# Expert stage of a top-4 mixture: output stores move from ScalarE's DMA queue to SyncE's, TensorE reads its expert numbers per product group, loop bodies go from 48 to 24 steps

## The chip, the cores and the metric

The kernel runs on one core of a Trainium2 chip. The metric is the device time of one execution in microseconds (us); the figure that counts is the median of several runs. TensorE is called PE in the profile, VectorE DVE, ScalarE ACT, GpSimd POOL and SyncE SP; a "q" behind a name (SPq, ACTq) is that engine's queue of DMA instructions.

## The reference

The input is 8 sequences of 1024 rows of 256 numbers, 8192 rows in all. What is computed, cut to its core:

```python
x = x + time_and_channel_mix(layernorm(x))            # first half, 16 tiles of 512 rows
xt = layernorm(x).reshape(-1, 256)                     # 8192 rows
gates = sigmoid(xt @ expert_sel.T)                     # 32 experts
val, idx = top_k(gates, 4)
scores = relu(einsum('nd,edf->nef', xt, keys)) * gate_full[:, :, None]    # keys: 32 x 256 x 128
out = einsum('nef,efv->nv', scores, values)            # values: 32 x 128 x 256
return x + out
```

The first half is a layer norm, a recurrence over the rows of a sequence with four 256x256 projections, an output projection, a second norm and a two-layer mix of width 1024. The kernel computes the products of each row for its four chosen experts only.

## The kernel before

**The mixing stage** works through 16 tiles of 512 rows. Each engine has a list of its own for a tile; four tiles are written out, then a loop of two tiles per pass runs five times, then the rest is written out. At the end of each tile POOL scatters the 512 x 4 rows (each row to four experts) with 16 indirect DMAs (L1340) into `lists`, a table in DRAM in which each block of 128 rows ("unit") belongs to one expert. DVE keeps the plan: which expert each unit has (`plan_expert`), and, for the first 48 units, which are worked off in another order, where they lie (`plan_row`) and where their results go (`plan_store`).

**The expert stage** is `expert_phase` (from L1396). 288 units are taken two at a time, which makes 144 steps; one step's 256 rows are a batch. All five engines run the same step list, each shifted:

- SP loads batch i at its step i (`rows`, L1474): 256 KB from `lists` to one of six homes `xr`. In the first 24 batches (the head) it reads two row numbers from `plan_row` into registers (L1457) and issues two DMAs of 128 KB (L1479); later it issues one DMA (L1483). Ahead of that it waits until DVE has finished step i-6 (L1501). SP also loads the residual tiles (`load_resid`, L1486) and stores the finished tiles (`store_tile`, L1492), one of each per 8 steps.
- PE at its step i does the first product of batch i-2 (`inner`, L1553: eight matmuls against `keys`), transposes batch i (`turn_rows`, L1575), transposes the hidden rows of batch i-4 (`turn_sums`, L1588) and does the second product of batch i-6 (`outer`, L1597: six matmuls against `values`). Which expert's weights these use comes out of `plan_expert` through registers: `experts_of` (L1540) reads them for four steps at a time, eight registers, once for the keys and once for the values. Both reads of four steps fall in the same step.
- ACT waits for PE's step (L1660) and then copies four results out of PSUM: L1663, L1666 (`xt_hi`), L1669, and L1676, which writes the output `y` of batch i-6 into one of four homes. At the start of its next step it stores that batch (`store`, L1642): in the head two register reads and two DMAs of 128 KB (L1648), later one DMA of 256 KB (L1651), all on ACT's own DMA queue. Before L1676 it waits until the batch four earlier has landed in `sorted_rows`.
- DVE has three instructions per step (L1717, L1720, L1726), of which L1720 (`xt_lo`) allows PE the first product two steps on, and from step 36 on two weighted sums (L1707) per step. Four groups of 128 rows, eight steps, make one output tile.
- POOL gathers, per tile, 16 times 128 rows of `sorted_rows` (L1758), four for each group of 128 rows. It starts on tile n when batches up to 8n+23 have landed (L1753), and for each group waits until DVE has summed the group four earlier (L1755), since `ye` has four homes.

The loops: SP, ACT, PE and DVE each write out 48 steps, then loop over 48 steps twice, then write out the rest:

```python
SPAN = 6 * RING                                   # RING = 8
for i in range(SPAN): step(i, i % SPAN, i // SPAN)
with pe.Fori(1, NSTEPS // SPAN) as pair:          # NSTEPS = 144
```

POOL's list has no loop here.

Of the kernel before, what the change touches and what calls it, by code (L numbers as in the profile page):

```python
# [44 lines left out]
UNIT = P  # L45
# [26 lines left out]
SUM_LAG = 36  # L72
OUT_AT = SUM_LAG + RING + HOMES[0] * WIDE
RESID_AT = OUT_AT - 20
PLAN_STEP, FIRST_RESIDS, KEYS_FIRST = 2, 14, 7
OPEN_BELOW = (UNIT - 1) / UNIT

# [1318 lines left out]
def expert_phase(nc, scope, sem, g):  # L1396
# [32 lines left out]
    (pe_step, low_ready, xhi_ready, x_ready, sums_ready, hhi_ready, h_ready, ycopy_ready, sum_step) = (  # L1429
        sem(n) for n in "pe_step low_ready xhi_ready x_ready sums_ready hhi_ready h_ready ycopy_ready sum_step".split())  # L1430

    SPAN = 6 * RING
    BATCHES = SPAN // WIDE
    HEAD_BATCHES = HEAD_END // FOLD
    SUM_END = SUM_LAG + 2 * NT * J
    HELD = 4
    PART_OF = P // FOLD
    assert NSTEPS % SPAN == 0 and SPAN % HELD == 0 and SPAN // RING % RESIDS == 0 and HEAD_END <= SUB * SPAN
    assert all(BATCHES % homes == 0 and HEAD_BATCHES % homes == 0 for homes in (XB, YB))

    def within(i, first, end):

        return not isinstance(i, int) or first <= i < end

    def in_head(b):

        return isinstance(b, int) and b < HEAD_BATCHES
# [25 lines left out]
    def on_sync(sp):  # L1473
        def rows(b, r):  # L1474

            q = r % XB
            if in_head(b):
                for n, at in enumerate(held_rows(sp, plan_row, b * FOLD, LIST_ROWS - UNIT)):
                    sp.dma_start(xr[n * PART_OF:(n + 1) * PART_OF, q],  # L1479
                                 lists[bass.ds(at, UNIT), :].rearrange("(p f) d -> p f d", f=FOLD)  # L1480
                                 ).then_inc(rows_loaded[q], 16)
            else:
                sp.dma_start(xr[:, q], lists[bass.ds(b * (FOLD * UNIT), FOLD * UNIT), :]  # L1483
                             .rearrange("(p f) d -> p f d", f=FOLD)).then_inc(rows_loaded[q], 16)

        def load_resid(tile, q, nth):  # L1486

            after(sp, out_stored[q], 16 * nth)
            sp.dma_start(resid[:, q], residual[bass.ds(tile * TILE, TILE), :].rearrange("(p j) d -> p j d", j=J)
                         ).then_inc(resid_loaded[q], 16)  # L1490

        def store_tile(tile, q):  # L1492

            sp.wait_ge(sum_step, TOPK * J * (tile + 1))
            sp.dma_start(out[bass.ds(tile * TILE, TILE), :].rearrange("(j p) d -> p j d", p=P), resid[:, q]
                         ).then_inc(out_stored[q], 16)

        def step(i, r, pair):
            if r % WIDE == 0 and within(i, 0, NSTEPS):
                b = BATCHES * pair + r // WIDE  # L1500
                after(sp, x_ready, i - (XB - 1) * WIDE)  # L1501
                rows(b, r // WIDE)
            for at, act_on in ((OUT_AT, store_tile), (RESID_AT, load_resid)):
                if (r - at) % RING == 0 and within(i, at, at + NT * RING):
                    n = (r - at) // RING
                    tile, q, nth = (SPAN // RING) * pair + n, n % RESIDS, (SPAN // RING // RESIDS) * pair + n // RESIDS
                    if act_on is store_tile:
                        store_tile(tile, q)
                    elif not (isinstance(tile, int) and tile < RESIDS):
                        load_resid(tile, q, nth)  # L1510

        sp.wait_ge(head_ready, 1)
        sp.wait_ge(scattered[0], 16 * NT // 2 * J * TOPK)
        sp.wait_ge(scattered[1], 16 * (NT // 2 - 1) * J * TOPK)
        for i in range(SPAN):
            if i == RING:
                sp.wait_ge(last_scattered, 16 * J * TOPK)
            step(i, i % SPAN, i // SPAN)
            if i == FIRST_RESIDS:
                sp.wait_ge(places_ready, 1)  # L1520
                for tile in range(RESIDS):
                    load_resid(tile, tile, 0)
        with sp.Fori(1, NSTEPS // SPAN) as pair:
            for r in range(SPAN):
                step(SPAN * pair + r, r, pair)
        for i in range(NSTEPS, OUT_AT + (NT - 1) * RING):
            step(i, i % SPAN, i // SPAN)
        last = (NT - 1) % RESIDS
        for j in range(J):
            G = (NT - 1) * J + j  # L1530
            sp.wait_ge(sum_step, TOPK * (G + 1))
            sp.dma_start(out[G * P:(G + 1) * P, :], resid[:, last, j, :]).then_inc(out_stored[last], 16)
        for q in range(RESIDS):
            tiles = len(range(q, NT, RESIDS))
            sp.wait_ge(out_stored[q], 16 * (tiles - 1 + J if q == last else tiles))

    def on_tensor(pe):
        held = {}

        def experts_of(b, r, use):  # L1540

            n = r % HELD
            if n == 0 or (use, r) not in held:
                _, found = nc.values_load_multi_w_load_instructions(
                    plan_expert[0:1, bass.ds(b * SUB, (HELD - n) * SUB)], engines=(pe.engine,), min_val=0,
                    max_val=E - 1,
                    skip_runtime_bounds_check_because="the plan writes all of the table, bounded, ahead of its "
                                                      "semaphores")
                for m in range(HELD - n):
                    held[use, r + m] = found[m * SUB:(m + 1) * SUB]  # L1550
            return held.pop((use, r))

        def inner(i, r, pair):  # L1553

            b, q = i - H_LAG, r - H_LAG
            experts = experts_of(b, q, "keys")
            pe.wait_ge(x_ready, SPAN * pair + q // WIDE * WIDE + WIDE)
            after(pe, sums_ready, b - 1)
            for s, e in enumerate(experts):
# [37 lines left out]
        def outer(i, r):  # L1597

            b, q = i - Y_LAG, r - Y_LAG
            experts = experts_of(b, q, "values")  # L1600
            pe.wait_ge(h_ready, b + 1)
            after(pe, ycopy_ready, b - 1)
            for s, e in enumerate(experts):
                v_hi, v_lo = (values[:, bass.ds(e, 1), h].rearrange("p a w -> p (a w)") for h in range(2))
                cols = ps[:, Y + q % 2, s * D:(s + 1) * D]
                c = slice(s * P, (s + 1) * P)
                pe.matmul(cols, h_hi[:, q % HS, c], v_hi, start=True, stop=False)  # L1607
                pe.matmul(cols, h_hi[:, q % HS, c], v_lo, start=False, stop=False)
                mm = pe.matmul(cols, h_lo[:, q % HS, c], v_hi, start=False, stop=True)  # L1609
            return mm  # L1610
# [19 lines left out]
                pe.wait_ge(values_split, LOADS)  # L1630
            step(i, i % SPAN, i // SPAN)
        pe.wait_ge(plan_ready, 1)
        held.clear()
        with pe.Fori(1, NSTEPS // SPAN) as pair:
            for r in range(SPAN):
                step(SPAN * pair + r, r, pair)
        held.clear()
        for i in range(NSTEPS, NSTEPS + Y_LAG):
            step(i, i % SPAN, i // SPAN)

    def on_scalar(act):
        def store(b, r):  # L1642

            q = r % YB
            act.wait_ge(ycopy_ready, (b + 1) * WIDE)
            if in_head(b):
                for n, at in enumerate(held_rows(act, plan_store, b * FOLD, LIST_ROWS - FOLD * UNIT + FOLD - 1)):
                    act.dma_start(sorted_rows[bass.ds(at, UNIT, FOLD), :], y[:, q, n, :]  # L1648
                                  ).then_inc(y_stored[q], 16)
            else:  # L1650
                act.dma_start(sorted_rows[bass.ds(b * (FOLD * UNIT), FOLD * UNIT), :]  # L1651
                              .rearrange("(p f) d -> p f d", f=FOLD), y[:, q]).then_inc(y_stored[q], 16)

        def step(i, r, pair):
            done = r - Y_LAG - 1
            if done % WIDE == WIDE - 1 and within(i, Y_LAG + WIDE, NSTEPS + Y_LAG + 1):
                store(BATCHES * pair + done // WIDE, done // WIDE)
            if not within(i, 0, NSTEPS + Y_LAG):
                return
            act.wait_ge(pe_step, i + 1)  # L1660
            if within(i, H_LAG, NSTEPS + H_LAG):
                q = r - H_LAG
# [16 lines left out]
        act.wait_ge(head_ready, 1)  # L1679
        for stored in x1_stored:  # L1680
            act.wait_ge(stored, 16 * NT // 2)
        for i in range(SPAN):
            step(i, i % SPAN, i // SPAN)
        with act.Fori(1, NSTEPS // SPAN) as pair:
            for r in range(SPAN):
                step(SPAN * pair + r, r, pair)
        for i in range(NSTEPS, NSTEPS + Y_LAG + 1):
            step(i, i % SPAN, i // SPAN)

    def on_vector(dve):  # L1690
# [38 lines left out]

        split_keys(dve, KEYS_FIRST, LOADS)  # L1730
        split_values(dve, 0, 1)
        for i in range(SPAN):
            if i == PLAN_STEP:
                plan_later(dve)
            if i == PLAN_STEP + 2:
# [3 lines left out]
                split_values(dve, 2 * i + 1, min(2 * i + 3, LOADS))  # L1739
            if i == PLAN_STEP + 2:  # L1740
                places_sorted(dve)
        with dve.Fori(1, NSTEPS // SPAN) as pair:
            for r in range(SPAN):
                step(SPAN * pair + r, r, pair)
        for i in range(NSTEPS, SUM_END):
# [65 lines left out]
```

## Time and profile before

| | |
|---|---|
| runs | 1259.62, 1264.01, 1264.49 us; median 1264.01 |
| profiled execution | 1261.35 us; its span, first to last instruction, 1259.5 us |
| busy over the span | PE 1107.5 us (88%), DVE 1015.1 (81%), POOL 760.8 (60%), ACT 752.8 (60%) |
| mean granted clock of TensorE | 0.958 |
| moved by DMA | 227.55 MB, mean 181 GB/s |
| expert stage | first xt_lo (L1720) at 811.7 us, last at 1213.1 us; last gather issued at 1252.48 us |

The shares are means over two stages with different limits. The mixing stage, which the change leaves alone, fills the first 810 us; the expert stage is the rest, and it is read by stretches. Times in the rows are us from the span's start, unless marked ns.

### The profile page before, as it was taken

The page shows a single profiled execution, that of the slowest core. Times are in us where ns is not written, and L with a number is a line of the kernel's source. Part 1 is how long each engine was busy: PE and PEld are TensorE (multiplying, and loading weights), DVE is VectorE, ACT ScalarE, POOL GpSimd, SP SyncE. Part 2 cuts the span into 40 slices and gives each one's busy share as a digit, 9 for nine tenths or more (in the row PEclk, how much of TensorE's full clock was granted, in tenths as well). Part 3 has the DMA queues.
Part 4 walks back from the last instruction along what each step waited for, and adds up shares of the span by engine and source line. Part 5 has one row for each costly group of instructions (what it writes and reads, how often), then busy time and mean ns, then how long its engine had stood idle before and what let it go on. Part 6 is the DMA issues. An engine that isn't in the chain of part 4 may idle for free.

```text
span 1259.5 us, 24103 instructions
## 1 busy us (share of the span) xinstructions
PE 1107.5 (88%) x6830; PEld 953.2 (76%) x6831; DVE 1015.1 (81%) x2268; ACT 752.8 (60%) x1504; POOL 760.8 (60%) x868
## 2 busy tenths in 40 slices
PE   6799999999999999999999997377799898799870
PEld 6678888788787887887787876377799898689860
DVE  3788899899899898899899885864478888678874
ACT  4467567567568567567568557444566566456550
POOL 2434377568558558668568666620077777657776
PEclk9799999999999999999999999589999999899995
DMA  9422134234224323324322128356599999899994
GB/s 342 153 85 101 39 130 141 85 110 142 96 96 146 108 79 137 102 94 145 102 87 80 65 75 350 129 181 204 160 307 348 356 356 350 292 310 360 346 315 126
DMA packets 131134, 227.55 MB, mean 181 GB/s; under 512 B 15584, under 2 KB 74976, under 8 KB 129632
## 3 DMA queue, kind: packets, MB, share of 16 engines
q1 hardware_dynamic: 82272, 121.49, 28.1%
q0 software_dynamic: 24576, 67.14, 16.1%
q10 hardware_dynamic: 24192, 37.76, 8.0%
q8 instruction: 48, 0.79, 0.3%
q14 instruction: 46, 0.38, 0.1%
HBM read 100.50 MB, written 125.83 MB: 180 GB/s over the span
## 4 chain that ended last, share of the span: by engine, by line
POOL 29%; PE 20%; issue 18%; DVE 13%; ACT 8%; DMA 7%; ACTq 3%; POOLq 1%; DVEq 0%; SPq 0%
POOL lists L1340 13%; PE ps L452 7%; POOL ye L1758 6%; DMA ye<-sorted_rows,place_of 5%; PE ps L1567 2%; POOL th_r L1383 2%; POOL rs L1294 2%; POOL xp L1370 2%; ACTq L1648 2%; DVE resid L1707 2%; PE ps L1584 2%; DVE xp L998 1%; ACT xt_hi L1666 1%; ACT y L1676 1%; DVE stats L880 1%
## 5 line engine op out<-in xcount | busy, mean ns | idle before, releaser
L1758 POOL DMA_INDIRECT ye<-sorted_rows,place_of x256 | 247.9, 968 | 176.6 <-DMA sorted_rows<-y 88.9
L1707 DVE SCALAR_TENSOR_TENSOR resid<-ye,gates,resid 128x256 f32<-128x256 f32 x256 | 123.1, 481 | 78.1 <-DMA ye<-sorted_rows,place_of 36.9
L1567 PE MATMUL ps<-keys,xt_hi 128*128 x576 | 149.7, 337 | 37.7 <-DVE xt_lo L1720 28.9
L1340 POOL DMA_INDIRECT lists<-rows_even,slot x128 | 142.8, 1115 | 46.0 <-issue 40.3
L1340 POOL DMA_INDIRECT lists<-rows_odd,slot x128 | 138.8, 1085 | 47.0 <-issue 40.3
L1663 ACT ACTIVATE sums<-ps 128x256 f32<-128x256 f32 x144 | 55.3, 384 | 170.9 <-PE ps L1609 122.7
L1567 PEld LDWEIGHTS ps<-keys,xt_hi 128*128 128x128 f32 x576 | 111.2, 193 | 48.8 <-issue 48.5
L1040 DVE TENSOR_TENSOR k_lo<-ksq,k_hi 128x512 fp32r<-128x512 f32 x128 | 117.5, 934 | 18.3 <-ACT k_hi L778 18.2
L1570 PE MATMUL ps<-keys,xt_lo 128*128 x576 | 129.9, 226 | 0.0
L769 ACT ACTIVATE kr<-ps,bias_k 128x512 f32<-128x512 f32 x128 | 86.7, 683 | 47.2 <-PE ps L452 44.5
L1570 PEld LDWEIGHTS ps<-keys,xt_lo 128*128 128x128 f32 x576 | 112.7, 196 | 0.0
L452 PE MATMUL ps<-xn1t_hi,wt_hi 128*128 128x512 f32 x256 | 104.1, 407 | 6.4 <-DVE xn1t_lo L892 4.9
L1085 DVE RECIPROCAL u<-u 128x512 f32<-128x512 f32 x32 | 106.8, 3337 | 0.0
L452 PE MATMUL ps<-xn2t_hi,wk_hi 128*128 128x512 f32 x256 | 103.8, 406 | 2.8 <-ACT kr L769 0.8
L1607 PE MATMUL ps<-values,h_hi 128*128 x288 | 94.2, 327 | 11.3 <-issue 6.1
L659 PE MATMUL ps<-k_hi,wv_hi 128*128 128x512 f32 x256 | 103.4, 404 | 0.0
L452 PE MATMUL ps<-xn2t_hi,wk_lo 128*128 128x512 f32 x256 | 101.5, 396 | 0.0
L1720 DVE TENSOR_TENSOR xt_lo<-ps,xt_hi 128x512 fp32r<-128x512 f32 x144 | 98.8, 686 | 3.2 <-ACT xt_hi L1666 2.3
L452 PE MATMUL ps<-xn2t_lo,wk_hi 128*128 128x512 f32 x256 | 101.3, 396 | 0.0
L452 PE MATMUL ps<-xn1t_hi,wt_lo 128*128 128x512 f32 x256 | 101.1, 395 | 0.0
L452 PE MATMUL ps<-xn1t_lo,wt_hi 128*128 128x512 f32 x256 | 101.1, 395 | 0.0
L661 PE MATMUL ps<-k_hi,wv_lo 128*128 128x512 f32 x256 | 100.5, 393 | 0.0
(213 smaller groups left out, 3229.3 us busy)
## 6 DMA issues: line engine op xcount, KB each, us to landing
lists<-zeros SPq DMA_DIRECT2D x18, 2048.0 KB, 10.3
xr<-lists SPq DMA_DIRECT2D x120, 256.0 KB
sorted_rows<-y ACTq DMA_DIRECT2D x120, 256.0 KB
x_sb<-in_x SPq DMA_DIRECT2D x16, 512.0 KB, 4.4
residual<-xp SPq DMA_DIRECT2D x16, 512.0 KB, 5.1
experts_raw<-in_expert_in SPq DMA_DIRECT2D x8, 1024.0 KB, 15.1
resid<-residual SPq DMA_DIRECT2D x16, 512.0 KB, 7.4
out_dram<-resid SPq DMA_DIRECT2D x15, 512.0 KB, 6.5
```

The costliest lines, as they stand in the source:

```text
L452: mm = pe.matmul(bank, w(k), m(k), start=n == 0, stop=n == last)
L659: pe.matmul(bank, wv_hi[:, f, c], k_hi[:, f, :], start=f == 0, stop=False, skip_group_check=True)
L661: pe.matmul(bank, wv_lo[:, f, c], k_hi[:, f, :], start=False, stop=False, skip_group_check=True)
L1040: dve.tensor_tensor(k_lo[:, m, :], ksq[:, m % KRING, :], k_hi[:, m, :].bitcast(F32), ALU.subtract).then_inc(klo_ready, 1)
L1085: dve.reciprocal(u[:, m, :], u[:, m, :]).then_inc(rden_ready, 1)
L1340: pool.indirect_dma_start(lists, bass.IndirectOffsetOnAxis(ap=slot[:, q, n:n + 1], axis=0), rows[q][:, n // TOPK, :], None).then_inc(last_ ...
L1567: pe.matmul(cols, xt_hi[:, home, c], keys[:, bass.ds(e, 1), k].rearrange("p a h w -> p (a h w)"), start=k == 0, stop=False, skip_group_che ...
L1570: mm = pe.matmul(cols[:, 0:DE], xt_lo[:, home, c], keys[:, bass.ds(e, 1), k, 0].rearrange("p a w -> p (a w)"), start=False, stop=k == KD - ...
L1607: pe.matmul(cols, h_hi[:, q % HS, c], v_hi, start=True, stop=False)
L1707: dve.scalar_tensor_tensor(acc, ye[:, j, k, :], gate, acc, ALU.mult, ALU.add).then_inc(sum_step, 1)
L1720: dve.tensor_tensor(xt_lo[:, r % XTS], ps[:, XT + r % 2, :], xt_hi[:, r % XTS].bitcast(F32), ALU.subtract).then_inc(x_ready, 1)
L1758: pool.indirect_dma_start(ye[:, j, k, :], None, sorted_rows[0:(tile + 3) * OPENED * UNIT, :], bass.IndirectOffsetOnAxis(ap=place_of[:, n:n ...
```

## The change

Three edits, all in `expert_phase`:

1. `store` moves from ACT to SP. SP issues the store of batch i-12 in its step i, behind the load of batch i and ahead of the tile store and the residual load; the wait for `ycopy_ready` moves with it. ACT has no DMA left in this stage.
2. `experts_of` reads two registers for one step, once ahead of each first product and once ahead of each second product.
3. `SPAN` is 24. PE writes out 24 steps and loops over 24 steps five times; SP, ACT and DVE write out 48 steps and loop over 24 steps four times.

The diff, cut to its core:

```diff
+STORE_LAG = HOMES[0] + Y_LAG
...
-    SPAN = 6 * RING
+    SPAN = 3 * RING
...
-    HELD = 4
...
+        def store(b, r):
+
+            q = r % YB
+            sp.wait_ge(ycopy_ready, (b + 1) * WIDE)
+            if in_head(b):
+                for n, at in enumerate(held_rows(sp, plan_store, b * FOLD, LIST_ROWS - FOLD * UNIT + FOLD - 1)):
+                    sp.dma_start(sorted_rows[bass.ds(at, UNIT, FOLD), :], y[:, q, n, :]
+                                  ).then_inc(y_stored[q], 16)
+            else:
+                sp.dma_start(sorted_rows[bass.ds(b * (FOLD * UNIT), FOLD * UNIT), :]
+                              .rearrange("(p f) d -> p f d", f=FOLD), y[:, q]).then_inc(y_stored[q], 16)
...
                 rows(b, r // WIDE)
+            if within(i, STORE_LAG, NSTEPS + STORE_LAG):
+                store(i - STORE_LAG, r - STORE_LAG)
...
-        for i in range(SPAN):
+        for i in range(2 * SPAN):
...
-        with sp.Fori(1, NSTEPS // SPAN) as pair:
+        with sp.Fori(2, NSTEPS // SPAN) as pair:
...
-        def experts_of(b, r, use):
-
-            n = r % HELD
-            if n == 0 or (use, r) not in held:
-                _, found = nc.values_load_multi_w_load_instructions(
-                    plan_expert[0:1, bass.ds(b * SUB, (HELD - n) * SUB)], engines=(pe.engine,), min_val=0,
...
-            return held.pop((use, r))
+        def experts_of(b):
+
+            _, found = nc.values_load_multi_w_load_instructions(
+                plan_expert[0:1, bass.ds(b * SUB, SUB)], engines=(pe.engine,), min_val=0, max_val=E - 1,
...
+            return found
...
-            experts = experts_of(b, q, "keys")
+            experts = experts_of(b)
...
-            experts = experts_of(b, q, "values")
+            experts = experts_of(b)
...
     def on_scalar(act):
-        def store(b, r):
...
         def step(i, r, pair):
-            done = r - Y_LAG - 1
-            if done % WIDE == WIDE - 1 and within(i, Y_LAG + WIDE, NSTEPS + Y_LAG + 1):
-                store(BATCHES * pair + done // WIDE, done // WIDE)
-            if not within(i, 0, NSTEPS + Y_LAG):
-                return
             act.wait_ge(pe_step, i + 1)
...
-        for i in range(SPAN):
+        for i in range(2 * SPAN):
             step(i, i % SPAN, i // SPAN)
-        with act.Fori(1, NSTEPS // SPAN) as pair:
+        with act.Fori(2, NSTEPS // SPAN) as pair:
```

DVE's loop is changed as ACT's.

## Rows read from the trace of the kernel before

**Rows 1.** Stretches: us, busy (x instructions) of PE, PEld, DVE, ACT, POOL, clock, DMA share, GB/s.

```profile
260.00:640.00 380.00, 370.81 (x1968) 302.27 (x1967) 342.23 (x748) 248.00 (x455) 257.56 (x308) 1.00 0.32 111
...
860.00:910.00 50.00, 38.76 (x310) 35.68 (x309) 21.53 (x45) 24.57 (x60) 0.00 (x0) 1.00 0.52 161
...
948.00:1077.00 129.00, 117.11 (x986) 112.59 (x986) 105.72 (x248) 80.91 (x198) 96.64 (x100) 1.00 1.01 354
```

**Rows 2.** The page's costliest groups: POOL's gathers (busy, mean ns, idle before).

```profile
L1758 POOL DMA_INDIRECT ye<-sorted_rows,place_of x256 | 247.9, 968 | 176.6 <-DMA sorted_rows<-y 88.9
```

**Rows 3.** Timeline of POOL: the first gather.

```profile
913.25 0.98 POOL L1758 DMA_INDIRECT ye<-sorted_rows,place_of  x1 [84.31 <-DMA sorted_rows<-y]
```

**Rows 4.** Timeline of POOL: its two long waits behind the loops' turn.

```profile
1091.32 0.95 POOL L1758 DMA_INDIRECT ye<-sorted_rows,place_of  x1 [2.46 <-DVE resid L1707]
...
1108.83 0.95 POOL L1758 DMA_INDIRECT ye<-sorted_rows,place_of  x1 [7.45 <-DVE resid L1707]
```

**Rows 5.** Timeline: ACT's store in a step of the head, and the head's last store.

```profile
868.83 0.62 ACT L1676 ACTIVATE y<-ps 128x512 f32<-128x512 f32 x1
...
870.13 0.85 ACTq L1648 DMA_DIRECT2D sorted_rows<-y  x2
...
871.03 0.39 ACT L1663 ACTIVATE sums<-ps 128x256 f32<-128x256 f32 x1 [1.58 <-issue]
...
909.21 0.84 ACTq L1648 DMA_DIRECT2D sorted_rows<-y  x2
```

**Rows 6.** Timeline of ACT behind the head: its copy of y and the store.

```profile
1160.37 0.62 ACT L1676 ACTIVATE y<-ps 128x512 f32<-128x512 f32 x1
1161.15 0.36 ACTq L1651 DMA_DIRECT2D sorted_rows<-y  x1
```

**Rows 7.** Timeline of SP's queue: pairs of head loads, and three loads from step 8 on.

```profile
810.53 1.12 SPq L1479 DMA_DIRECT2D xr<-lists  x2
...
812.33 1.12 SPq L1479 DMA_DIRECT2D xr<-lists  x2
...
832.57 2.28 SPq L1479 DMA_DIRECT2D xr<-lists  x3
```

**Rows 8.** Timeline around PE's step 126, which reads (DVE steps 125, 126 and 127).

```profile
1165.06 0.68 DVE L1720 TENSOR_TENSOR xt_lo<-ps,xt_hi 128x512 fp32r<-128x512 f32 x1
...
1166.70 0.38 PE L1607 MATMUL ps<-values,h_hi 128*128 x1 [0.96 <-DVE h_lo L1726]
...
1168.62 0.69 DVE L1720 TENSOR_TENSOR xt_lo<-ps,xt_hi 128x512 fp32r<-128x512 f32 x1
...
1170.92 0.67 DVE L1720 TENSOR_TENSOR xt_lo<-ps,xt_hi 128x512 fp32r<-128x512 f32 x1
```

**Rows 9.** Timeline at the turn of the 48-step loops (DVE steps 95 and 96).

```profile
1077.38 0.68 DVE L1720 TENSOR_TENSOR xt_lo<-ps,xt_hi 128x512 fp32r<-128x512 f32 x1
...
1082.57 0.58 PE L1567 MATMUL ps<-keys,xt_hi 128*128 x1 [6.20 <-issue]
...
1087.80 0.68 DVE L1720 TENSOR_TENSOR xt_lo<-ps,xt_hi 128x512 fp32r<-128x512 f32 x1
```

**Rows 10.** DMA of 260 to 640 us: every queue (packets, MB, share of 16 engines), even scatters.

```profile
q1 hardware_dynamic: 21888, 25.17, 19.2%
q0 software_dynamic: 6240, 17.05, 12.3%
...
lists<-rows_even,slot POOLq DMA_INDIRECT x66, 2.5
```

**Rows 11.** DMA of 820 to 1220 us: SP's queue, ACT's queue, an instruction queue.

```profile
q1 hardware_dynamic: 29250, 51.26, 38.3%
...
q10 hardware_dynamic: 23573, 36.64, 24.5%
q8 instruction: 32, 0.52, 0.5%
```

**Rows 12.** DMA of 10 to 20 us: SP's queue, the only one at work then.

```profile
q1 hardware_dynamic: 2152, 4.00, 104.3%
```

More of the change, by code:

```diff
@@ L1435, in expert_phase @@
     SUM_END = SUM_LAG + 2 * NT * J
-    HELD = 4
     PART_OF = P // FOLD
-    assert NSTEPS % SPAN == 0 and SPAN % HELD == 0 and SPAN // RING % RESIDS == 0 and HEAD_END <= SUB * SPAN
+    assert NSTEPS % SPAN == 0 and SPAN // RING % RESIDS == 0 and HEAD_END <= SUB * SPAN
     assert all(BATCHES % homes == 0 and HEAD_BATCHES % homes == 0 for homes in (XB, YB))
@@ L1537, in on_tensor @@
     def on_tensor(pe):
-        held = {}
-        def experts_of(b, r, use):
-            n = r % HELD
-            if n == 0 or (use, r) not in held:
-                _, found = nc.values_load_multi_w_load_instructions(
-                    plan_expert[0:1, bass.ds(b * SUB, (HELD - n) * SUB)], engines=(pe.engine,), min_val=0,
[L1546 to L1550, printed above, removed]
-            return held.pop((use, r))
+        def experts_of(b):
+            _, found = nc.values_load_multi_w_load_instructions(
+                plan_expert[0:1, bass.ds(b * SUB, SUB)], engines=(pe.engine,), min_val=0, max_val=E - 1,
+                skip_runtime_bounds_check_because="the plan writes all of the table, bounded, ahead of its "
+                                                  "semaphores")
+            return found
         def inner(i, r, pair):
             b, q = i - H_LAG, r - H_LAG
-            experts = experts_of(b, q, "keys")
+            experts = experts_of(b)
             pe.wait_ge(x_ready, SPAN * pair + q // WIDE * WIDE + WIDE)
@@ L1632, in on_tensor @@
         pe.wait_ge(plan_ready, 1)
-        held.clear()
         with pe.Fori(1, NSTEPS // SPAN) as pair:
@@ L1636, in on_tensor @@
                 step(SPAN * pair + r, r, pair)
-        held.clear()
         for i in range(NSTEPS, NSTEPS + Y_LAG):
@@ L1641, in on_scalar @@
     def on_scalar(act):
-        def store(b, r):
[L1644 to L1652, printed above, removed]
-        def step(i, r, pair):
-            done = r - Y_LAG - 1
-            if done % WIDE == WIDE - 1 and within(i, Y_LAG + WIDE, NSTEPS + Y_LAG + 1):
-                store(BATCHES * pair + done // WIDE, done // WIDE)
-            if not within(i, 0, NSTEPS + Y_LAG):
-                return
+        def step(i, r, pair):
             act.wait_ge(pe_step, i + 1)
@@ L1681, in on_scalar @@
             act.wait_ge(stored, 16 * NT // 2)
-        for i in range(SPAN):
+        for i in range(2 * SPAN):
             step(i, i % SPAN, i // SPAN)
-        with act.Fori(1, NSTEPS // SPAN) as pair:
+        with act.Fori(2, NSTEPS // SPAN) as pair:
             for r in range(SPAN):
                 step(SPAN * pair + r, r, pair)
-        for i in range(NSTEPS, NSTEPS + Y_LAG + 1):
+        for i in range(NSTEPS, NSTEPS + Y_LAG):
             step(i, i % SPAN, i // SPAN)
@@ L1731, in on_vector @@
         split_values(dve, 0, 1)
-        for i in range(SPAN):
+        for i in range(2 * SPAN):
             if i == PLAN_STEP:
@@ L1741, in on_vector @@
                 places_sorted(dve)
-        with dve.Fori(1, NSTEPS // SPAN) as pair:
+        with dve.Fori(2, NSTEPS // SPAN) as pair:
             for r in range(SPAN):
```

## The prediction

> **What bounds the kernel now.** I read the stretches first, because the page's shares mix two stages. The mixing stage takes the first 810 us and stays as it is, so only the expert stage counts, and it has two parts with different limits. In the head, 860 to 910 us, PE ran 310 matmuls in 50 us, 20 per step, so a step takes 3.2 us, and the DMA engines are half busy at 161 GB/s. From 948 to 1077 us 986 matmuls took 129 us, 2.62 us per step; there the DMA share is 1.01 at 354 GB/s, PE is busy 91% [rows 1].
>
> POOL's gathers show what sets the end. 256 gathers of 968 ns mean, 0.30 us apart, need 256 x 1.268 = 324.6 us [rows 2]; the first starts at 913.25 [rows 3]. All that POOL then lost is 15.8 us (176.6 idle, less 84.3 before the first gather, less 255 x 0.30) [rows 2, 3], so the chain ends at 1253.7, and 9.3 of the 15.8 lie in two waits, 2.46 and 7.45 us less the usual 0.30 each, both for DVE's sums just after the loops' turn [rows 4]. So the expert stage is a head that decides when POOL starts, a POOL chain that nearly never rests, and 6 us behind the last gather. PE, at 2.30 us per undisturbed step [rows 8] (18.4 us per tile against POOL's 16 x 1.268 = 20.3), is not the bound but must not fall behind. A piece of work saved on PE or ACT is worth something only if it lets POOL start earlier or takes a wait from it.
>
> **Part 1, the store on SP: the head.** A head step of ACT: its copy of y ends at 869.45, the two stores are issued from 870.13 to 870.98, and the next copy starts at 871.03 after 1.58 us of idling by "issue" [rows 5]. Behind the head the store starts 0.16 us after the copy [rows 6], against 0.68 here, so two register reads cost 0.52. ACT's 2.0 us of copies plus 1.2 more give the 3.2 us: ACT paces the head, and that weight goes. But SP takes it up. A pair of head loads with its reads takes SP 1.80 us (pairs start at 810.53 and 812.33) [rows 7]. With the store, between 0.52 + 0.85 = 1.37 and again 1.80, I take 1.58, what it costs ACT now. Working down SP's list: its step 8 starts at 832.57 now, held by the last scatter, and will again [rows 7]; steps 8 to 11 take 4 x 1.80 = 7.2; steps 12 to 23 hold a load pair and a store pair, 12 x 3.38 = 40.6, worse than the 3.2 of now; the three first residual loads, which SP issues behind its step 14, add 2.0 (an estimate from the 0.65 us at which the two loads of a pair follow each other, 0.65 + 0.47 = 1.12); steps 24 to 34 have one load (0.45) and a store pair, 11 x 2.03 = 22.3, and step 35 adds 0.45 + 0.52. The pair of batch 23 is issued at 832.57 + 7.2 + 40.6 + 2.0 + 22.3 + 1.0 = 905.7, against 909.21 now [rows 5]. POOL waits for this store, so it starts 3.5 us earlier. With the two bounds for the store pair, 24 x 0.22 = 5.3 us either way: 9 us earlier to 2 us later. ACT's spare time is worth no more, because SP is the pacer of steps 12 to 23.
>
> Behind the head SP has one load, one store and, every eighth step, a tile store and a residual load: some 0.4 us each, under 1 us per 2.5 us step. Queued behind the store's wait for y is the next load, which waits for DVE's step one later anyway, five steps ahead of need; a residual load that waits for its home would now hold up stores too, but its home's store left four steps, 10 us, before. Zero, hidden by these leads. Loads and stores now share SP's queue: 38.3% + 24.5% of the engines' time, 88 MB in 400 us or 220 GB/s [rows 11]. The queue has alone moved 4.00 MB in 10 us, 400 GB/s [rows 12], so zero again; if that cover were wrong, batches would land late and POOL would wait.
>
> The Trainium skill (Perfetto Trace Analysis, DMA Optimizations) speaks against this edit: with loops it advises one engine to issue inputs and another outputs. By that rule the head's 3.5 us would be lost and more; no row here shows such a cost.
>
> **Part 2, the reads.** PE's step 126, with its 16 registers, made DVE's step 3.56 us long against 2.30 for the next, 0.96 of it ahead of the second product [rows 8]. So a group costs PE up to 1.3 us in four steps. Now each step has two reads of two registers. ACT pays 0.52 for one, so 1.04 per step, bounded by nothing exposed and all of it exposed (2.30 + 1.04 = 3.3 us per step). I take nothing exposed: the keys' read falls behind the dispatch of the second product, the values' read while the 1.4 us of first product and transposes run. PE's step becomes even, 2.3. As POOL needs 2.54 per step, this gives the end about 1 us in small waits. Late next is POOL itself.
>
> **Part 3, the loops.** At the loops' turn DVE's step 96 starts 10.42 us after step 95, PE idling 6.20 us by "issue" [rows 9]: 8.1 us too much. POOL pays for it with its 9.3 us in the steps behind it [rows 4]. Is the cost in the turn or in the length? The mixing loop answers. In 260 to 640 us only q1 and q0 carry packets: no instructions were fetched through 66 / 16 = 4.1 passes [rows 10], and PE ran 1968 matmuls, some 480 per pass, at 98% busy [rows 1]. The expert loop has 48 x 20 = 960 matmuls, and in its stretch q8 fetches 32 packets of instructions [rows 11]. A body of 24 steps has 480, the size of the mixing loop's. So I expect its turns to be free and the fetches to stop: POOL gets back 9.3 us.
>
> The Trainium skill (Runtime: NRT & Kernel Launch, Instruction fetch mechanics) says that a taken branch outside a window of two pages forces a fetch before work goes on. By it the mixing loop too would fetch at each turn, which rows 10 contradict; taken as it stands it makes the first rival below.
>
> **Sum.** 3.5 + 1 + 9.3 = 13.8 us off 1261.35 us, the profiled execution's own time (1259.5 span and 1.85 around it): 1247.6. The median of the runs, 1264.01, stands 2.7 us above that execution, so 1250.
>
> **Rivals.** *The turns cost what this one costs (slower).* The place is PE's turn after steps 48, 72, 96 and 120. If a turn always fetches, POOL pays 9.3 us four times instead of once: 1264 - 3.5 - 1 + 3 x 9.3 = 1287. It decides from about 4 us per turn, where 4 x 4 eats the gain. For it: the one turn seen under full DMA cost that much. Against it: rows 10. Chance 0.11.
>
> *The reads are exposed.* If a read of two registers costs PE as much as one of eight, or 1.04 us lies bare, a step takes 2.9 to 3.3 us. At 3.0, 114 steps behind the head take 342 us from 905 on, then 48 us for the last batches, 16 gathers and the end: span 1295, median 1300. It ends slower from 2.7 us per step on, what the steps average now. Against it: ACT's 0.52 us. The Trainium skill (DMA: Bandwidth & Descriptors, Latency and other measured facts) gives a register load a floor near 0.6 us and says that loads are grouped to spread it; by that figure PE would carry 1.2 us per step. Chance 0.09.
>
> *The gain is taken elsewhere.* Between 948 and 1077 us the DMA engines are full at 354 GB/s. A tile moves 7.3 MB (16 x 128 KB gathered, 8 x 256 KB each way, two of 512 KB), 20.7 us at that rate against POOL's 20.3. What the stall left idle is then needed, 13 tiles x 0.4 = 5 us; if the head gains nothing as well, 1264 - 5 = 1259. Chance 0.15.
>
> *The loop bodies still fetch though the turn is cheap, or SP's queue delays the stores:* 1262 to 1275. Chance 0.07.
>
> **Numbers.** Forecast 0.58, its own range 1240 to 1257: head 5.3 either way, and the 15.8 us of POOL's waits as the most that can go. Range 1238 to 1276: it takes in the third and fourth case and leaves out the first two, 0.20 together. A measurement tells 0.5%, 6 us, from no change: faster than 1257.7 is 0.65 (forecast, and part of the third case), within 0.12, slower 0.23.
>
> **What would show it.** Right: no ACTq row in the stage; first gather at 908 to 914 us; head steps uneven, near 2.3 us, then near 3.4 while SP issues both pairs, then 2.3; the reads' 1 us gaps gone; no step of 10 us; under 16 packets on q8; POOL's idle near 163 us against 176.6. Wrong: PE idle by "issue" at steps 48, 72, 96 or 120 (first rival); steps near 3 us throughout (second); POOL waiting for sorted_rows often (third and fourth).

## The result: slower by 6.2%

The changed kernel takes 1340.78 us (median of 4 runs, 1338.56 to 1350.4), the kernel before 1264.25 us beside it; the ratio is 1.0624, 95% interval 1.0563 to 1.0685. The profiled execution took 1341.97 us with a span of 1340.1.

### The profile after

POOL's gathers on the page:

```profile
L1746 POOL DMA_INDIRECT ye<-sorted_rows,place_of x256 | 247.6, 967 | 257.1 <-DMA sorted_rows<-y 132.9
```

The gathers cost the same; POOL idles 257.1 us where it idled 176.6 [rows 2], 80.5 more, and the span grew by 80.6. On POOL's timeline:

```profile
914.85 0.98 POOL L1746 DMA_INDIRECT ye<-sorted_rows,place_of  x1 [85.53 <-DMA sorted_rows<-y]
...
1051.54 0.94 POOL L1746 DMA_INDIRECT ye<-sorted_rows,place_of  x1 [7.41 <-DMA sorted_rows<-y]
```

The first gather comes 1.6 us later than before [rows 3]. From then on 14 waits of 4.7 to 7.6 us such as the one at 1051.54 follow, nearly one per tile. The stretches (columns as in [rows 1]) tell who is late:

```profile
860.00:910.00 50.00, 42.29 (x305) 38.56 (x304) 22.62 (x48) 25.71 (x63) 0.00 (x0) 0.92 0.58 182
948.00:1077.00 129.00, 95.83 (x746) 86.79 (x744) 81.47 (x188) 61.74 (x152) 71.83 (x75) 1.00 0.84 264
```

From 948 to 1077 us PE ran 746 matmuls where it ran 986 [rows 1], at a granted clock of 1.00 in both; the DMA share fell from 1.01 to 0.84, so neither the DMA engines nor POOL are the bound: PE's steps are late. On DVE's timeline, 119 steps behind the head (24 to 143, from 893.22 to 1294.90) average 3.38 us; before it was 2.70 (from 891.81 to 1213.12). The difference of the two stretches, 80.4 us, is the whole loss. PE's timeline shows the place, at a slow step and at a quick one (last second product of a step, first key product of the next):

```profile
1055.23 0.28 PE L1616 MATMUL ps<-values,h_lo 128*128 x1
1056.48 0.38 PE L1574 MATMUL ps<-keys,xt_hi 128*128 x1 [0.97 <-issue]
...
1111.12 0.28 PE L1616 MATMUL ps<-values,h_lo 128*128 x1
1111.81 0.38 PE L1574 MATMUL ps<-keys,xt_hi 128*128 x1 [0.41 <-issue]
```

The gap stands ahead of the key products, where the keys' experts are read. In the kernel before, these products follow with no gap in an undisturbed step:

```profile
1169.66 0.28 PE L1609 MATMUL ps<-values,h_lo 128*128 x1
1169.78 0.28 PE L1567 MATMUL ps<-keys,xt_hi 128*128 x1
```

And the reads themselves are in the trace, as instructions of PE's sequencer (not counted as busy, so in no list of costly groups). Asked for by its source line, the read answers with duration min/median/max in ns; first the kernel after, a quick stretch (1109 to 1127 us) and a slow one (1020 to 1048):

```profile
L1554 PEldq TENSOR_LOAD <-plan_expert x12: 536/548/650, 1109.6 to 1125.7; - x12
...
L1554 PEldq TENSOR_LOAD <-plan_expert x15: 540/1109/1408, 1020.5 to 1046.1; - x15
```

then the kernel before, 925 to 1200 us:

```profile
L1544 PEldq TENSOR_LOAD <-plan_expert x56: 333/1020/2391, 925.0 to 1196.9; - x56
```

A read of two registers takes 0.54 us at best and 1.1 as the median of the slow stretch. The long ones stand where the gap is: from 925 to 1200 us, 43 of the 80 reads ahead of the key products last over 0.9 us, and 7 of the 81 ahead of the value products. The last row was there to be read before the prediction, and it was not read.

One slow step shows how the time adds up. The first key product starts at 1052.83 and the next step's at 1056.48, 3.65 us later. In between stand the values' read and the keys' read (L1554 from 1053 to 1057 us):

```profile
L1554 PEldq TENSOR_LOAD <-plan_expert x2: 547/840/1132, 1053.7 to 1055.1; - x2
```

They last 0.55 and 1.13 us; the other 1.97 us are the rest of the step's issue. During the first read PE went on with a key product and the transposes issued ahead of it, with no gap; during the second only the last value products were left, and the 0.97 us gap followed.

The instruction queues from 820 to 1220 us answer to [rows 11]:

```profile
q1 hardware_dynamic: 44384, 72.78, 55.8%
...
q8 instruction: 10, 0.16, 0.2%
```

10 packets on q8 instead of 32; and at step 96, a turn, DVE's pitch is 3.86 us where it was 10.42 [rows 9].

### The profile page after: what moved, and what is told of

It reads as the page before. It is cut to its first block, busy times and chain, and to the rows that moved or that the text cites. A ratio compares the mean times of both kernels' runs of the same rounds, so it can differ in the third digit from the quotient of the medians.

```text
span 1340.1 us, 24452 instructions
## 1 busy us (share of the span) xinstructions
PE 1137.9 (85%) x6830; PEld 965.1 (72%) x6831; DVE 1017.7 (76%) x2268; ACT 753.6 (56%) x1504; POOL 762.5 (57%) x868
## 4 chain that ended last, share of the span: by engine, by line
PE 38%; POOL 23%; issue 18%; DVE 12%; ACT 4%; DMA 2%; SPq 1%; POOLq 1%; DVEq 0%; ACTq 0%
POOL lists L1341 12%; PE ps L1574 9%; PE ps L453 8%; PE ps L1591 4%; PE ps L1614 3%; PE ps L1577 2%; PE ps L1616 2%; PE ps L1615 2%; POOL rs L1295 2%; PE ps L1601 2%; POOL th_r L1384 2%; DVE resid L1695 2%; POOL xp L1371 2%; DVE xp L999 1%; DVE stats L881 1%
## 5 line engine op out<-in xcount | busy, mean ns | idle before, releaser
L1746 POOL DMA_INDIRECT ye<-sorted_rows,place_of x256 | 247.6, 967 | 257.1 <-DMA sorted_rows<-y 132.9
L1574 PE MATMUL ps<-keys,xt_hi 128*128 x576 | 159.3, 354 | 93.7 <-issue 50.0
L1591 PE MATMUL ps<-consts,xr 128*128 128x128 f32 x576 | 93.4, 287 | 11.5 <-DMA xr<-lists 11.5
L1705 DVE TENSOR_TENSOR sums<-ps,sums 128x256 f32<-128x256 f32 x144 | 60.3, 419 | 55.3 <-ACT sums L1651 55.3
L1664 ACT ACTIVATE y<-ps 128x512 f32<-128x512 f32 x144 | 88.5, 615 | 24.4 <-DMA sorted_rows<-y 22.3
```

What stands on the lines that cost most here:

```text
L1574: pe.matmul(cols, xt_hi[:, home, c], keys[:, bass.ds(e, 1), k].rearrange("p a h w -> p (a h w)"), start=k == 0, stop=False, skip_group_che ...
L1591: mm = pe.transpose(into.rearrange("p (t f) -> p f t", f=FOLD)[:, f, :], xr[:, b % XB, f, k * P:(k + 1) * P], ident)
L1664: act.activation(y[:, home, units].rearrange("p s d -> p (s d)"), ps[:, Y + q % 2, :], ACT.Copy).then_inc(ycopy_ready, 1)
L1746: pool.indirect_dma_start(ye[:, j, k, :], None, sorted_rows[0:(tile + 3) * OPENED * UNIT, :], bass.IndirectOffsetOnAxis(ap=place_of[:, n:n ...
```

## The experiments

### One part undone, or one part alone

e1 puts the reads back in groups of four into the changed kernel:

```
-            experts = experts_of(b)
+            experts = experts_of(b, q, "keys")      # HELD = 4, as before; likewise "values"
```

> The kernel after with the reads put back in groups of four batches (8 registers per read, two reads in four steps). Theory A (each two-register read lies bare in PE's stream, 0.6 to 1.3 us per step): the loss goes, the undisturbed step is 2.3 us again, and the store on SyncE and the loops of 24 give what was forecast for them, 1248 to 1258 us. Rival B (the stores in SyncE's queue cost the time): 1320 us or more, steps still 2.9 to 3.7 us. Rival C (the loops' turns cost it): over 1290 us, with PE idle by issue at the turns.

Measured: 1263.65 us, ratio 0.9986 (0.9968 to 1.0004). The loss goes, as A said; but the time is above A's 1248 to 1258 us: the store and the loops together are worth nothing that can be told from zero.

e2 is the kernel before with only the reads of the change.

> The kernel before with only the reads of two registers per batch. A: steps of 2.9 to 3.7 us, 1330 to 1350 us. B and C: within 0.5% of before, 1258 to 1270 us.

Measured: 1372.51 us, ratio 1.0839 (1.082 to 1.0858): the reads alone cost 107 us, 31 more than the whole change and more than A's 1330 to 1350. B and C are out. Its loops still have 48 steps, with one DVE step of 11.38 us at the turn; that is 8 us of the 31. The rest comes with longer reads (the table below). Against the changed kernel, e2 has longer loops and its stores on ScalarE; which of the two makes the reads longer no run tried.

e3 is the kernel before with only the stores on SyncE (the `store` function, its call and STORE_LAG of the diff).

> The kernel before with only the stores on SyncE's queue. A: the head is up to 3.5 us shorter or equal (in the changed kernel the first gather came at 914.85, 1.6 us later than before), the rest as before: 1258 to 1266 us. B: 1320 us or more.

Measured: 1277.77 us, ratio 1.01 (1.0083 to 1.0117). Outside both expectations: the store does cost something, 12.6 us here, though far from all.

e4 is the kernel before with only the loops (SPAN = 3 * RING, and 2 * SPAN steps ahead of the loops of SP, ACT and DVE).

> The kernel before with only loops of 24 steps. A: the stall of 9.3 us at the one turn is replaced by turns of 1 us or less: 1253 to 1258 us. C: each of the four turns of PE stalls it by 4 us or more: over 1280 us.

Measured: 1255.65 us, ratio 0.9918 (0.99 to 0.9936). As A said: 9.5 us between the medians (by the interval, 8 to 13), against the 9.3 that POOL lost to the one long turn. Its DVE timeline at steps 95 and 96, which answers to [rows 9]:

```profile
1081.75 0.69 DVE L1720 TENSOR_TENSOR xt_lo<-ps,xt_hi 128x512 fp32r<-128x512 f32 x1
...
1084.90 0.67 DVE L1720 TENSOR_TENSOR xt_lo<-ps,xt_hi 128x512 fp32r<-128x512 f32 x1
```

3.15 us over the turn instead of 10.42. The profiled execution of e4, at 1259.58 us the longest of its six, is only 1.8 us shorter than the profiled one of the kernel before: the two waits of [rows 4] are gone, but POOL has others, 3.68 us at 1001.71 the longest. So the trace shows that the turn is cheap, and only the medians show the 9.5 us.

### What a read costs

Two kernels change how much a read holds, two how many batches a group has.

```
 e5: found = experts_of(i - Y_LAG, Y_LAG - H_LAG + 1)   # one read of 10 registers per step
 e6: plan_expert[0:1, bass.ds(b * SUB, 3 * SUB)]        # two reads of 6, four registers unused
 e7: HELD = 2 on e1        e8: HELD = 8 on e1          # batches per read
```

> The changed kernel with one read per step in the place of two: ten registers in one instruction (the experts of the five batches from the values' to the keys'), of which the first two and the last two are used. Theory A (the price is of the read instruction, about 0.6 us or more, whatever it loads, and PE's step is the time to issue its matmuls plus its reads): half the reads, steps of 2.3 to 2.7 us, 1262 to 1300 us. Rival D (the price is of the register, 0.25 to 0.35 us each, from 4 registers per step for 0.6 to 1.3 us): ten registers, steps over 4.5 us, over 1500 us.

Measured: 1419.35 us, ratio 1.1193 (1.1114 to 1.1272). Neither: half the reads, and 79 us more.

> The changed kernel with two reads per step as before it, but of six registers each (four of them unused). A: nothing changes, 1332 to 1352 us. D: twelve registers per step instead of four, over 1500 us.

Measured: 1515.33 us, ratio 1.1954 (1.1883 to 1.2026). As D said, over 1500.

> The changed kernel with reads of four registers for two batches, so two read instructions in two steps. A: as the joint read, one instruction per step, 1262 to 1300 us. D: the number of registers is the same, 1341 us.

Measured: 1262.91 us, ratio 0.9972 (0.9942 to 1.0002). A. The two theories have one hit each, so neither is the law.

> The changed kernel with reads of sixteen registers for eight batches, two read instructions in eight steps. A: half the stalls of groups of four (e1), which POOL's chain hides for the most part: 1255 to 1264 us, same or slightly faster than e1. D: same as e1 or longer, as each group stalls PE by 5 us: 1263 to 1280 us.

Measured: 1263.45 us, ratio 0.9975 (0.9947 to 1.0002), the same as e1; it does not decide.

e9 gives the changed kernel's reads four registers each, e10 adds a third read of two.

```
 e9:  plan_expert[0:1, bass.ds(b * SUB, 2 * SUB)]
 e10: for s, e in enumerate(experts):
+         if s == 1:
+             e = experts_of(b)[1]
```

> The changed kernel with two reads per step of four registers each (two of them unused). From DVE's steps 24 to 143 the mean step is 3.38 us with reads of 2 registers, 4.68 with two reads of 6, 4.05 with one read of 10. Theory L (linear: a price per read plus 0.16 us per register, which these three fit with 0.32 us per read): 4.0 us per step, 1341 + 136 x 0.65 = 1429 us. Theory F (floor: about 1.15 us for any read of up to 4 registers, 0.3 us per register above, and only 1 us of a step for issuing the matmuls; it alone explains why reads of four registers in every second step, e7, cost nothing): unchanged, 3.4 us per step, 1335 to 1365 us.

Measured: 1368.57 us, ratio 1.0831 (1.0798 to 1.0864). Between L and F: 3.6 us above F's range and 60 below L.

> The changed kernel with a third read of two registers in each step, between the key products of the two experts (it reads the same two again). F: another 1.15 us per step, 1341 + 136 x 1.15 = 1497 us. L: another 0.64 us per step, 1428 us. If the reads overlapped with the products there (third theory: the reads cost only where they stand, ahead of the first key product): under 1360 us.

Measured: 1423.11 us, ratio 1.1256 (1.1222 to 1.1291). Near L's 1428; F is out, and so is the theory that only the place counts.

e13 reads once per step (found = experts_of(i - H_LAG) for both products, so the second product is with the experts of a later batch), e14 reads twice at one place:

```
 e14: found = experts_of(i - Y_LAG) + experts_of(i - H_LAG)   # both ahead of the keys
```

> The changed kernel with one read of two registers per step in the place of two: the value products use the experts that the key products of the same step use, four batches ahead, so the second products are with the wrong experts. Counting reads in units of up to four registers, the mean step behind 925 us is 3.39 us with two units (changed kernel), 4.04 and 4.06 with three (e5, e10), 4.66 with four (e6): 0.65 us per unit. Theory U (every unit lies bare): 2.74 us per step, at every step a gap of 0.3 us or more ahead of the first key product, 1262 to 1275 us. Theory V (one unit per step fits behind the products, only the second lies bare): steps at 2.25 us between POOL's waits, 1253 to 1264 us, as e1.

Measured: 1268.58 us, ratio 1.003 (1.0008 to 1.0051), in U's range and outside V's. Its PE timeline has a gap at ordinary steps, though 0.2 us and not the 0.3 or more that U wanted:

```profile
1096.32 0.38 PE L1573 MATMUL ps<-keys,xt_hi 128*128 x1 [0.20 <-issue]
...
1099.06 0.38 PE L1573 MATMUL ps<-keys,xt_hi 128*128 x1 [0.22 <-DVE xt_lo L1711]
```

> The changed kernel with both reads of a step issued one behind the other, ahead of the key products, in the place of one ahead of the keys and one ahead of the values. U: the place does not matter, 1341 us within 10. Rival P (a read costs by what stands in PE's queue where it is issued; the values' read is hidden now, the keys' is not): both lie bare behind the same six matmuls, 1400 us or more.

Measured: 1339.51 us, ratio 1.0583 (1.0562 to 1.0604). As U said: for the kernel's time the place makes no difference, and P falls.

The guesses about floors and units were needless, for the durations stand in the traces. The same row of each kernel, 925 to 1200 us:

e2 (two reads of two registers per step):

```profile
L1539 PEldq TENSOR_LOAD <-plan_expert x149: 535/557/2507, 925.7 to 1200.0; - x149
```

e7 (two of four in every second step):

```profile
L1559 PEldq TENSOR_LOAD <-plan_expert x101: 328/379/1730, 925.7 to 1197.3; - x101
```

e9 (two of four):

```profile
L1554 PEldq TENSOR_LOAD <-plan_expert x152: 332/1004/2172, 924.8 to 1198.5; - x152
```

e10 (three of two):

```profile
L1554 PEldq TENSOR_LOAD <-plan_expert x203: 530/545/1569, 924.4 to 1199.3; - x102
```

e5 (one of ten):

```profile
L1554 PEldq TENSOR_LOAD <-plan_expert x69: 1077/2672/3294, 923.3 to 1198.0; - x69
```

e6 (two of six):

```profile
L1554 PEldq TENSOR_LOAD <-plan_expert x118: 819/1471/2325, 924.4 to 1198.5; - x118
```

e13 (one of two):

```profile
L1554 PEldq TENSOR_LOAD <-plan_expert x100: 532/870/2247, 924.6 to 1199.0; - x100
```

e14 (two of two, together):

```profile
L1554 PEldq TENSOR_LOAD <-plan_expert x164: 534/549/1884, 924.8 to 1198.5; - x164
```

Adding up every read's duration that starts from 925 to 1200 us, and dividing by the DVE steps that start there, gives this (275 us over the number of steps is the mean step):

| kernel | read time per step | mean step | difference |
|---|---|---|---|
| before (55 reads, 102 steps) | 0.54 | 2.70 | |
| e1, e7, e8 | 0.57, 0.58, 0.54 | 2.70, 2.70, 2.72 | |
| e13 one read | 0.98 | 2.78 | 1.80 |
| e14 together | 1.50 | 3.35 | 1.85 |
| after (161 reads, 80 steps) | 1.56 | 3.44 | 1.88 |
| e9 four registers | 1.74 | 3.62 | 1.88 |
| e2 only reads | 1.76 | 3.72 | 1.96 |
| e10 third read | 2.13 | 4.04 | 1.91 |
| e5 joint | 2.26 | 4.04 | 1.78 |
| e6 wide | 2.77 | 4.66 | 1.89 |

From one read per step up, a step lasts its read time plus 1.8 to 1.96 us. PE's sequencer is then the bound: about 1.9 us to issue the step's 20 matmuls with their address steps and waits, and nothing else while a register read runs. The 1.9 us are what is left over in the table, and the 1.97 of the step shown above agrees. PE's array needs some 2.25 us per step, and POOL, with its waits, leaves 2.70 (before, e1). So read time is free while it and the 1.9 us stay below that pace. At 0.98 us per step (e13) the kernel is 5 us slower than with groups of four (e1); from there on, 1.79 us more of reading per step (e6) make the step 1.88 us longer, so all of it is paid. For the joint read this holds although it is one instruction, since that one lasts 2.26 us on average.

### Where the store's price lies

e11 and e12 are e4 with the stores of batches 0 to 23, or those from 24 on, on SyncE:

```
 e11 (SP): if isinstance(i, int) and STORE_LAG <= i < HEAD_BATCHES + STORE_LAG:
               store(i - STORE_LAG, r - STORE_LAG)
 e12 (SP): if within(i, HEAD_BATCHES + STORE_LAG, NSTEPS + STORE_LAG):
               store(i - STORE_LAG, r - STORE_LAG)
```

> Only loops (e4) with the stores of the 24 head batches on SyncE and the later ones on ScalarE. Theory S (what SyncE costs is the delay of the later stores, 1.03 us behind the copy instead of 0.15, which POOL's gathers wait for): as e4, 1253 to 1259 us, the first gather within 1 us of 913. Rival H (the head on SyncE costs it): 1260 us or more.

Measured: 1250.62 us, ratio 0.9898 (0.9871 to 0.9926); 2.4 us below S's range, and its first gather is at 914.98, 1 us outside what S said. H is out.

> Only loops (e4) with the stores of the head on ScalarE and those of batches 24 to 143 on SyncE. S: POOL waits for sorted_rows as in e1, 1260 to 1266 us. H: as e4, 1253 to 1259 us.

Measured: 1264.62 us, ratio 0.9994 (0.9974 to 1.0014). S: the later stores take back all that the loops gave, the head's do not. The gathers of e4, e11 and e12 on their pages:

```profile
L1758 POOL DMA_INDIRECT ye<-sorted_rows,place_of x256 | 249.7, 976 | 173.2 <-DMA sorted_rows<-y 94.7
```
```profile
L1773 POOL DMA_INDIRECT ye<-sorted_rows,place_of x256 | 248.1, 969 | 163.9 <-DMA sorted_rows<-y 87.6
```
```profile
L1773 POOL DMA_INDIRECT ye<-sorted_rows,place_of x256 | 248.0, 969 | 178.8 <-DMA sorted_rows<-y 96.3
```

How a later store is delayed shows on the timelines of e4 (ACT's copy, then the store) and of e12 (two copies with SP's load and store):

```profile
1142.43 0.62 ACT L1676 ACTIVATE y<-ps 128x512 f32<-128x512 f32 x1
...
1143.21 0.35 ACTq L1651 DMA_DIRECT2D sorted_rows<-y  x1
```
```profile
1142.41 0.62 ACT L1691 ACTIVATE y<-ps 128x512 f32<-128x512 f32 x1
...
1144.07 0.33 SPq L1484 DMA_DIRECT2D xr<-lists  x1
...
1144.65 0.62 ACT L1691 ACTIVATE y<-ps 128x512 f32<-128x512 f32 x1
1144.66 0.35 SPq L1496 DMA_DIRECT2D sorted_rows<-y  x1
```

ACT sends the store 0.16 us behind the copy. On SP it goes 1.63 us behind the copy's end, after a load that waits for DVE. In e1, over the 114 stores behind 925 us, the mean is 1.01 us, 35 are over 1 us and the longest takes 4.89 (in e4: 0.15, none over 0.20). The last store of a tile is what POOL waits for. In the changed kernel itself the mean is 0.59 us and none is over 1 us: beside its longer steps the stores are hardly delayed.

e11 is faster than both kernels of the study: of POOL's 163.9 us idle, 85.1 lie ahead of the first gather and 255 x 0.30 = 76.5 between gathers, so 2.3 us of waits are left, against 15.8 before. Its interval meets that of e4, so that the head on SyncE adds anything is not shown.

e15 is e11 with HELD = 8.

> e11 (loops of 24, head stores on SyncE, the others on ScalarE) with reads for eight batches instead of four. POOL lost only 2.3 us behind its first gather in e11, so there is nothing left to gain: 1247 to 1253 us by every theory; over 1256 us if a group of sixteen registers stalls PE long enough for POOL to wait.

Measured: 1273.61 us, ratio 1.0075 (1.0055 to 1.0095), 23 us above e11. Its read time per step, 0.63 us, is below the 0.98 of e13, but it comes in lumps: DVE's steps 62, 70 and 78 last 5.3, 4.8 and 5.8 us, once per group, and POOL's timeline waits of this kind:

```profile
1157.53 0.94 POOL L1773 DMA_INDIRECT ye<-sorted_rows,place_of  x1 [4.31 <-DMA sorted_rows<-y]
...
1181.20 0.94 POOL L1773 DMA_INDIRECT ye<-sorted_rows,place_of  x1 [3.73 <-DMA sorted_rows<-y]
```

e8 has the same groups and lost nothing against e1. The traces show one difference: the reads ahead of the value products, most of sixteen registers, last 2.85 us (median) in e15 and 1.88 in e8. Why is open.

## Why the prediction was wrong, step by step

The forecast was 1250 us, some 14 us faster; the change made the kernel 76.5 us slower.

**The bound.** Right that, in the kernel before, POOL's chain set the end and that PE "must not fall behind". Wrong in how near PE was: by the array it had 18.4 us per tile against POOL's 20.3; by its sequencer it had 8 x (1.9 + 0.54) = 19.5.

**Part 2, the step that failed.** "I take nothing exposed." From ACT's 0.52 us I had the size of a read at its best nearly right (0.54). The upper bound, 3.3 us per step, is within 3% of the 3.38 measured, but partly by luck: the reads of a step last 1.56 us and not 1.04, and about 0.35 of it is hidden. I chose the lower end because matmuls run beside the reads. But what runs beside them is only what was issued ahead, and the sequencer had 0.35 us per step to spare (2.25 - 1.9), not a step's work. The row against it was [rows 8]: two reads of eight registers made one step 1.26 us longer. Asked for by its line from 1162 to 1167 us, the kernel before has these two:

```profile
L1544 PEldq TENSOR_LOAD <-plan_expert x2: 1017/1318/1619, 1162.6 to 1164.8; - x2
```

1.02 and 1.62 us, so about half of their time was bare already. With four steps to a group POOL hid it; with two reads in each step nothing does. The change did not split the same read time into smaller parts: eight registers in one read take 1.02 us for four batches, two take 0.77 on average for one batch, so the time per batch went from 0.25 to 0.77 us for each of the two uses.

The second rival was the outcome, at a chance of 0.09 and too low a price: with 3.38 in the place of 3.0 its own sum gives 905 + 114 x 3.38 + 48 = 1338 us of span. The Trainium skill (DMA: Bandwidth & Descriptors, Latency and other measured facts) has a floor of some 0.6 us for a register load; by it two loads are 1.2 us per step, and I set it aside for ACT's 0.52. The traces are near the page: 0.53 us at least for two registers, 0.75 to 0.87 on average in e14, the changed kernel and e2. It is no strict floor, as reads of four registers went down to 0.33.

**Part 3.** Right in mechanism, and in size by the medians. e4 gained 9.5 us where 9.3 were forecast (its one profiled execution shows 1.8, see above), the fetches fell from 32 packets to 10, and the first rival (each turn costs 9.3 us) is out. That PE's length of 480 matmuls is what counts, and not that of the other engines' loops, was not tried apart. By the traces' records a pass of PE's loop has some 2600 instructions with 48 steps (before) and 1350 with 24 (after), the mixing loop's 1010.

**Part 1, head.** Forecast 3.5 us earlier, with bounds from 9 earlier to 2 later; measured 1.6 later. Batch 23's store pair went out at 911.61 instead of 905.7. SP's head steps, on its timeline after:

```profile
867.08 1.15 SPq L1479 DMA_DIRECT2D xr<-lists  x2
868.92 0.86 SPq L1492 DMA_DIRECT2D sorted_rows<-y  x2
870.80 1.15 SPq L1479 DMA_DIRECT2D xr<-lists  x2
```

A load pair and a store pair repeat after 3.72 us, not 3.38: each pair takes SP 1.8 us or more, so the store pair belonged at its upper bound. And a queue was forgotten: the three first residual loads now stand in one queue with the stores, and y's home is late by that (SP's and ACT's timelines after):

```profile
849.44 1.41 SPq L1501 DMA_DIRECT2D resid<-residual  x3
```
```profile
858.67 0.60 ACT L1664 ACTIVATE y<-ps 128x512 f32<-128x512 f32 x1 [6.04 <-DMA sorted_rows<-y]
```

That copy waits for the store pair issued at 853.78, behind the three loads, which landed at about 858.65, 4.9 us later; the pair issued at 861.41 took 2.6. DVE's step 14 took 7.68 us there. I priced these loads at their issue, 2.0 us, and not at what their 1.5 MB does to a store behind them. That they are what delays it is argued from the order; no run moved them.

**Part 1, behind the head.** "Zero, hidden by these leads" failed. I counted the lead of the loads that stand behind a store, and not the store that stands behind a load: it has no lead, since its tile's gathers wait for it. e12 against e4 puts it at 9 us, e1 against e4 at 8, e3 against the kernel before at 12.6. The Trainium skill (Perfetto Trace Analysis, DMA Optimizations) advises separate engines for inputs and outputs in loops; e12 agrees for the later stores (1264.6 against 1255.7), e11 shows no such loss for the head's.

**The sum, by medians:** loops -9.5, stores about +8 (e1 against e4), reads +77 (the changed kernel against e1), together +76; measured +76.5. The three are steps of one way from the kernel before to the changed one, so they have to add up and prove nothing by it. In another order the parts differ: the reads alone cost 107 us on the kernel before (e2).

## What to carry to other kernels

A register read in PE's stream stops the issue of everything behind it, and PE's array can be "not the bound" while its sequencer is: add up the sequencer's instructions, reads among them, before calling anything there hidden. Ask the trace for the moved instruction by its own source line, in the kernel before; it may be in no list of busy groups. For a DMA moved to another queue, ask who waits for it as well as what it waits behind.

## What was not expected of the hardware

- The duration of a register read depends on more than its size. Reads of four registers lasted 0.38 us (median) in e7, where a pair comes every second step, and 1.00 in e9, where there are two per step; reads of two registers ahead of the key products lasted 0.54 us in one stretch of an execution and 1.1 to 1.4 in another, with the DMA share at 0.92 and 0.85 and the clock at 1.00 in both, while those ahead of the value products mostly stayed at 0.55. What sets this is open; no run isolated it. The 3.4 to 3.9 us steps of the changed kernel are those of the long reads: they hold 1.73 us of reads on average, the steps under 3.0 us 1.16.
- The whole read time per batch was the same in groups of two, four and eight (0.54 to 0.58 us per step in e7, e1, e8) and nearly three times as long in single batches (1.56).
- In e2, with loops of 48 steps and the stores on ScalarE, the same reads took longer, 1.76 us per step against 1.56; 119 x 0.2 = 24 us of the 31 by which e2 is above the whole change.
